# Layer 0 of a graph network: low sums through one bank, node ids in the other, packed count bounds

## The reference

```python
agg = segment_sum(x[src], dst, num_segments=12500)
h = x @ W_self + (agg * inv_deg[:, None]) @ W_neigh + b   # inv_deg = 1 / max(count of dst, 1)
# relu after layers 0 and 1; layer 0 takes layernorm(x)
x = x + h2                                                # the third layer's h
# routed: weights = LN(x) @ wr + br; the upper half of the nodes gets
# (gelu(LN(x) @ w1 + b1) @ w2 + b2) * weight; all rows: processed + LN(x) + x
```

## Time and profile before

| | |
|---|---|
| Median of 3 runs | 6063.86 us |
| The profiled execution | 6064.39 us, of which its span 6062.2 us |
| TensorE matmul, weight loads | 4166.2 us (69%), 2675.0 us (44%) |
| VectorE | 2811.4 us (46%) |
| ScalarE | 1056.5 us (17%) |
| GpSimd | 3912.0 us (65%) |
| Granted TensorE clock, mean | 0.862 |
| One-hots of layers 0 and 2 (L1155) | 3584 operations, 1013.8 us |
| One-hots of layer 1 (L1148) | 408 operations, 282.3 us |
| The chain that ended last | PE 24%, issue 23%, POOL 22%, DMA 9%, VectorE's sequencer 9%, VectorE 9% |

### The profile page before, as it was taken

The page is one execution under the profiler, slowest core; times in us unless marked ns, Lnnn a source line. Parts: engine busy times, 40 slices in busy tenths (PEclk is TensorE's granted clock), DMA queues, the critical chain, the costliest instruction groups (busy, mean ns, idle before and its releaser), DMA issues.

```text
span 6062.2 us, 112776 instructions
## 1 busy us (share of the span) xinstructions
PE 4166.2 (69%) x20492; PEld 2675.0 (44%) x20878; DVE 2811.4 (46%) x8126; ACT 1056.5 (17%) x2551; POOL 3912.0 (65%) x4094
## 2 busy tenths in 40 slices
PE   0444566666666667845778766666569999889992
PEld 0122233333333335523556433333257887667772
DVE  7223455555554445512222333344234445666666
ACT  7000011111111112200000100111012223334440
POOL 0777566665544447667777777776777765777760
PEclk9867788888888889976889988888689999999996
DMA  7555455555544446656777666666567775666655
GB/s 243 156 156 145 125 161 165 166 153 152 149 127 133 135 135 182 177 153 186 230 235 246 205 180 181 185 186 171 158 205 221 232 225 154 175 174 176 170 152 173
DMA packets 565085, 1065.85 MB, mean 176 GB/s; under 512 B 154587, under 2 KB 361983, under 8 KB 558527
## 3 DMA queue, kind: packets, MB, share of 16 engines
q0 software_dynamic: 261376, 803.21, 46.2%
q10 hardware_dynamic: 196564, 228.51, 11.0%
q1 hardware_dynamic: 106987, 32.54, 2.3%
HBM read 928.09 MB, written 135.83 MB: 175 GB/s over the span
## 4 chain that ended last, share of the span: by engine, by line
PE 24%; issue 23%; POOL 22%; DMA 9%; DVEq 9%; DVE 9%; ACT 2%; ACTq 1%; POOLq 0%; SPq 0%
POOL gath L619 22%; DMA gath<-table,idx_ring 7%; PE agg L826 6%; PE y L903 4%; PE hid L893 3%; DVE onehot L1155 3%; PE agg L828 3%; DVEq L1155 2%; DVEq L1214 2%; PE lo L765 2%; PE y L678 1%; DMA idx_ring<-idx_dram 1%; DVEq L1258 1%; PE count_ps L765 1%; ACTq L1502 1%
## 5 line engine op out<-in xcount | busy, mean ns | idle before, releaser
L619 POOL DMA_INDIRECT gath<-table,idx_ring x4084 | 3910.5, 958 | 1986.6 <-issue 1380.9
L826 PE MATMUL agg<-gath,onehot 128*128 x4831 | 1980.4, 439 | 985.0 <-SPq L546 799.6
L1155 DVE TENSOR_SCALAR onehot<-iota_row,window_base,dst_f 128x128 f32 x3584 | 1013.8, 360 | 1276.4 <-PE agg L828 478.3
L826 PEld LDWEIGHTS agg<-gath,onehot 128*128 x5216 | 560.4, 107 | 2122.0 <-issue 1788.3
L828 PE MATMUL agg<-gath,onehot 128*128 x3264 | 969.0, 297 | 184.6 <-SPq L546 139.9
L1148 DVE TENSOR_TENSOR onehot<-count_ps,dst_f 128x512 f32 x408 | 282.3, 692 | 827.7 <-PE agg L828 714.7
L903 PE MATMUL y<-w_sb,hidT 128*128 128x256 f32 x1568 | 368.6, 389 | 26.4 <-ACT hidT L1666 25.8
L828 PE MATMUL hid<-gath,onehot 128*128 x924 | 297.8, 322 | 122.4 <-SPq L546 105.6
L828 PEld LDWEIGHTS agg<-gath,onehot 128*128 x3264 | 338.6, 104 | 83.5
L828 PE MATMUL lo<-gath,onehot 128*128 x1028 | 342.0, 333 | 44.4 <-issue 18.9
L893 PE MATMUL hid<-featT,w_gnn 128*128 128x128 f32 x3136 | 366.9, 275 | 0.0
(11 more groups left out here) (182 smaller groups left out, 3962.1 us busy)
## 6 DMA issues: line engine op xcount, KB each, us to landing
gath<-table,idx_ring POOLq DMA_INDIRECT x4084
dense<-counts_dram ACTq DMA_DIRECT2D x50, 1024.0 KB, 6.4
table<-split ACTq DMA_DIRECT2D x194, 192.0 KB
counts_dram<-dense ACTq DMA_DIRECT2D x16, 1600.0 KB, 9.0
rows_f<-y ACTq DMA_DIRECT2D x194, 128.0 KB
dense<-rows_f ACTq DMA_DIRECT2D x48, 512.0 KB, 9.4
table<-gath ACTq DMA_DIRECT2D x24, 768.0 KB, 3.6
xb<-x ACTq DMA_DIRECT2D x97, 128.0 KB
```

The lines of the kernel that those rows point to most:

```text
L619: g.indirect_dma_start(gath[:, j, 0:PARTS * D], None, table[layer][:, :], bass.IndirectOffsetOnAxis(ap=idx_ring[:, h, i:i + 1], axis=0)).t ...
L826: mm(agg[p][:, 0:2 * D], oh, tile_rows[:, :, 0:2 * D], start=False, **flags)
L1155: last = v.tensor_scalar(onehot[:, bass.ds(pair, GROUP), :][:, j, :], iota_row[:], window_base[:, col(w)], dst_f[:, bass.ds(tiles, GROUP)] ...
```

## The change

Three edits, all in layer 0. (1) Low sums: both parities use one bank `lo0`; ScalarE copies it to `lo_sb[p]` in SBUF at the start of its slot (`lo_copied`); TensorE zeroes the bank for the next window only after that copy, and VectorE's `mean_done` reads the copy. (2) The half of `hid` that comes free takes the node ids, so that layer 0 makes a block's one-hots as layer 1 does. (3) The bounds of two groups are packed into one word (`group_pairs`), and each word's end is kept in a register for the next window, so that a turn of four windows needs 5 loads in place of 16. Beside them TensorE's `layer_product` waits for `self_ready` in place of `lo_ready`.

```diff
+        group_pairs = sb("group_pairs", [1, COUNT_GROUPS // 2 + 1], I32)
+        lo_sb = [sb(f"lo_sb{p}", [P, D + 1]) for p in range(2)]
...
-        agg_lo = [lo0[:], hid[:, 0, :]]
+        agg_lo = lo0[:]
-        window_ids = [count_ps[:, p * P:(p + 1) * P] for p in range(2)]
+        window_ids = [None if bank is None else [bank[:, p * P:(p + 1) * P] for p in range(2)]
+                      for bank in (hid[:, 0, :], count_ps[:], None)]
...
+        def group_bounds(eng):
+            ends = []
+            def end_of(value):
+                return eng.snap(value, min_val=0, max_val=TILES - 1)
+            def both_groups(turn, j):
+                def packed(k):
+                    return eng.value_load(group_pairs[0:1, col(turn * 4 + k)], min_val=0,
+                                          max_val=2 ** (2 * TILE_BITS) - 1)
+                if j == 0:
+                    ends[:] = [end_of(packed(0) >> TILE_BITS)]
+                here = packed(j + 1)
+                first, mid, end = ends[0], end_of(here & (2 ** TILE_BITS - 1)), end_of(here >> TILE_BITS)
+                ends[:] = [end]
+                return (first, mid), (mid, end)
+            return both_groups
...
                 if phase == 1 and (not isinstance(n, int) or n):
-                    pe.wait_ge(lo_ready, n)
+                    pe.wait_ge(self_ready, n)
...
                 if layer == 0:
-                    mm(agg_lo[p][:, 0:1], zeros[:], ones_bf[:, 0:1], start=True, **free)
+                    if not isinstance(n, int) or n:
+                        pe.wait_ge(lo_copied, n)
+                    mm(agg_lo[:, 0:1], zeros[:], ones_bf[:, 0:1], start=True, **free)
...
-                if layer == 1:
-                    v.tensor_scalar(window_ids[p], iota_row[:], window_base[:, col(w)], None,
-                                    ALU.add).then_inc(ids_ready, 1)
-                    dve.wait_ge(ids_ready, w - (DENSE - 1))
+                ids = window_ids[layer] and window_ids[layer][p]
+                if ids is not None:
+                    v.tensor_scalar(ids, iota_row[:], window_base[:, col(w)], None, ALU.add).then_inc(ids_ready, 1)
+                    dve.wait_ge(ids_ready, w + ((NT - DENSE) * layer + 1))
                     dve.sem_inc(dve_turn, 1)
...
-                    if layer == 1:
+                    if ids is not None:
                         v.tensor_tensor(onehot[:, bass.ds(pair, GROUP), :],
-                                        window_ids[p].unsqueeze(1).to_broadcast([P, GROUP, P]),
+                                        ids.unsqueeze(1).to_broadcast([P, GROUP, P]),
...
-                dve.wait_ge(agg_ready, n + 1)
-                v.tensor_scalar(deg[0:r, :], agg_lo[p][0:r, D:D + 1], 1.0, None, ALU.max).then_inc(deg_ready, 1)
+                dve.wait_ge(lo_copied, n + 1)
+                v.tensor_scalar(deg[0:r, :], lo_sb[p][0:r, D:D + 1], 1.0, None, ALU.max).then_inc(deg_ready, 1)
...
+                v.tensor_scalar(group_pairs[0:1, 1:COUNT_GROUPS // 2 + 1], group_tiles[0:1, :, 1], TILE_BITS, None,
+                                ALU.logical_shift_left).then_inc(groups_ready, 1)
+                dve.wait_ge(groups_ready, 9)
+                v.tensor_tensor(group_pairs[0:1, 1:COUNT_GROUPS // 2 + 1], group_pairs[0:1, 1:COUNT_GROUPS // 2 + 1],
+                                group_tiles[0:1, :, 0], ALU.bitwise_or).then_inc(groups_ready, 1)
...
+                    act.wait_ge(agg_ready, n + 1)
+                    if not isinstance(n, int) or n >= 2:
+                        act.wait_ge(mean_ready, n - 1)
+                    a.copy(lo_sb[1 - p][0:r, :], agg_lo[0:r, 0:D + 1]).then_inc(lo_copied, 1)
```

More of the change, by code:

```diff
@@ L87, in gnn_ffn_program @@
     COUNT_LOOPS = [(COUNT_AT, COUNT_END, 4), (COUNT_END, LAST_LOOPED, 2)]
+    TILE_BITS = TILES.bit_length()
     DENSE_LOOPS = [(DENSE_AT, DENSE_LAST, 2), (CLEAN, LAST_LOOPED, 2)]
@@ L301, in gnn_ffn_program @@
         lo_added = sem("lo_added")
+        lo_copied = sem("lo_copied")
         mid_added = sem("mid_added")
@@ L720, in count_ends, with count_group @@
                 nc.tensor.transpose(count_ps[0:1, 0:P], ends_count, ident[:]).then_inc(group_T, 1)
-            def count_group(g):
-                lo, end = pe_groups(g)
+            def count_group(g, bounds):
+                lo, end = bounds
                 (_, mid), _ = sub_spans(pe, lo, end, 2)
@@ L826, in block_products @@
                         mm(agg[p][:, 0:2 * D], oh, tile_rows[:, :, 0:2 * D], start=False, **flags)
-                        low = agg[p][:, 0:D] if layer else agg_lo[p][:, 0:lo_cols]
+                        low = agg[p][:, 0:D] if layer else agg_lo[:, 0:lo_cols]
                         last = mm(low, oh, tile_rows[:, :, 2 * D:2 * D + lo_cols], start=False, **flags)
@@ L847, in _ @@
                                    for blocks in (PAIRS - DENSE, PADDED_BLOCKS)] for layer in range(1, LAYERS)]
-            def pe_groups(g):
-                return [pe.value_load(group_tiles[0:1, col(g + i)], min_val=0, max_val=TILES - 1) for i in range(2)]
+            pe_groups = group_bounds(pe)
             def slot_layer0(w, half, p, part):
@@ L862, in slot_layer0 @@
                 if part and part[0] == 0:
+                    bounds = pe_groups(part[1], part[2])
                     first_half, *counting = [step for j in range(2) for step in
-                                             count_group(part[1] * 8 + (part[2] * 2 + j))]
+                                             count_group(part[1] * 8 + (part[2] * 2 + j), bounds[j])]
                     first_half()
@@ L1178, in mean_done @@
                 mean, inv = feat[p][0:r, :], inv_deg[0:r, col(n)]
-                v.tensor_scalar(mean, agg_lo[p][0:r, 0:D], inv, None, ALU.mult).then_inc(lo_added, 1)
+                v.tensor_scalar(mean, lo_sb[p][0:r, 0:D], inv, None, ALU.mult).then_inc(lo_added, 1)
                 dve.wait_ge(lo_added, n + 1)
@@ L1211, in aggregate_done @@
                                        ).then_inc(feat_ready if layer < 2 else o_ready, 1)
-            def dve_groups(g):
-                return [dve.value_load(group_tiles[0:1, col(g + i)], min_val=0, max_val=TILES - 1) for i in range(2)]
+            dve_groups = group_bounds(dve)
             def split_sources():
@@ L1229, in split_sources @@
                                 ALU.add).then_inc(groups_ready, 1)
-                v.memset(group_tiles[0:1, 0:1], 0).then_inc(groups_ready, 1)
+                v.memset(group_pairs[0:1, 0:1], 0).then_inc(groups_ready, 1)
                 dve.wait_ge(groups_ready, 7)
@@ L1242, in split_sources, with count_onehots @@
                 dve.wait_ge(group_T, 1)
-                v.tensor_copy(group_tiles[0:1, 1:COUNT_GROUPS + 1], count_ps[0:1, 0:COUNT_GROUPS]
+                v.tensor_copy(group_tiles[0:1, :, :].rearrange("p g t -> p (g t)"), count_ps[0:1, 0:COUNT_GROUPS]
                               ).then_inc(groups_ready, 1)
                 dve.wait_ge(groups_ready, 8)
+                v.tensor_scalar(group_pairs[0:1, 1:COUNT_GROUPS // 2 + 1], group_tiles[0:1, :, 1], TILE_BITS, None,
[3 more added lines that the diff above has]
+                                group_tiles[0:1, :, 0], ALU.bitwise_or).then_inc(groups_ready, 1)
+                dve.wait_ge(groups_ready, 10)
                 dve.sem_inc(count_copied, 2)
-            def count_onehots(g):
-                lo, end = dve_groups(g)
+            def count_onehots(g, bounds):
+                lo, end = bounds
                 (_, mid), _ = sub_spans(dve, lo, end, 2)
@@ L1255, in tile_onehots @@
                     slot = dve.snap((t + g) % COUNT_RING)
+                    tile = nc.s_assert_within(
+                        dve.snap(t), 0, TILES - 1,
+                        skip_runtime_bounds_check_because="tiles are counted from the sorted edges, below TILES")
                     dve.wait_ge(count_used, t + 2)
@@ L1280, in slot_layer0 @@
                 if part and part[0] == 0:
+                    bounds = dve_groups(part[1], part[2])
                     first_half, *counting = [step for j in range(2) for step in
-                                             count_onehots(part[1] * 8 + (part[2] * 2 + j))]
+                                             count_onehots(part[1] * 8 + (part[2] * 2 + j), bounds[j])]
                     first_half()
```

6 lines of the change are left out of this document (3 added, 3 removed).

## The result

The changed kernel took 5869.28 us, the median of 4 runs (5863.12 to 5874.99), the kernel before 6061.81 us in 4 runs on the same chip (6059.19 to 6067.04): a ratio of 0.9681, 95% interval 0.9664 to 0.9698, 192 us less. The forecast was 5873.

A forecast was written before the change was run, and what follows sets the result against it. VectorE's stream was taken to bound windows 6 to 69, gathers windows 70 to 97. Savings of 135 (late), 48 (early), 5, 3 and 1 us, less 1 for set-up, sum to 191: 6064.4 - 191 = 5873 us, range 5805 to 5965.

The forecast's parts named there:

- VectorE as the bound of the late stage: Layer 0, windows 22 to 69: VectorE's stream, sequencer included, sets the pace of these 1065 us; TensorE comes next.
- The late stage: Windows 22 to 69 of layer 0: VectorE's stream 149 us shorter (84 + 91 - 26), nine tenths reaching the end, 135 us.
- The blocks: One operation for a block's four one-hots in layer 0: 0.44 us saved per block, bounds 0.30 and 0.72.
- The loads: Packed bounds on VectorE in layer 0: 2.75 fewer register loads a window, 1.9 us saved each, bounds 0.9 and 2.2.
- The early stage: Windows 6 to 21 of layer 0: VectorE's stream 65 us shorter, 62 us of room above the gathers, 48 us taken.
- Setup, the first six windows, the last 28: Set-up costs 1 us; up to window 5, 3 and 5 us saved; windows 70 to 97, bound by gathers, 1 us saved.
- The copy costs nothing: ScalarE's added copy of low sums, about 0.40 us per window, is hidden by TensorE's products; about 1 us a window otherwise.
- The stops stay: The 15 stops of 5.7 to 6.7 us where VectorE's counting loop jumps back remain, the loop fetched anew each turn.
- Had they gone: Rival: VectorE's stops at the counting loop's jumps back go as well, 15 x 5.8 = 87 us more, 5786 us; chance 9 in 100.
- TensorE takes over early: Rival, counting stages: TensorE gives back only half of what VectorE saves, about 95 us, 5969 us; chance 12 in 100.
- One bank slower: Rival: ScalarE copies late, TensorE stands and GpSimd behind it; 3 us exposed per window, 6167 us; chance 3 in 100.
- nothing: Rival: VectorE's savings turn into waits for TensorE at the same places, no measurable change; chance 2 in 100.

The follow-up runs named there:

- f4: VectorE's loops over windows 6 to 69 of layer 0 hold two windows a turn instead of four, on the kernel before: 6016.78 us, ratio 0.9913.
- g1: Changed kernel with VectorE's loops over windows 6 to 69 holding two windows a turn instead of four, quick chip: 5838.75 us, 0.9627 of the kernel before.
- e3_bank: Kernel before with only the one bank for low sums and ScalarE's copy of it, slow chip: 7478.26 us, ratio 0.9992.
- f3b_copy_twice: Changed kernel with ScalarE copying the low sums out of the one bank twice per window of layer 0: 5875.15 us, 0.9689 of the kernel before.
- e4_selfwait: Kernel before with TensorE's layer_product of layer 0 waiting for self_ready in place of lo_ready, slow chip: 7463.02 us, ratio 0.9974.
- f0_after: The changed kernel itself, unedited, on a slow chip: 7280.31 us against 7454.13 for the kernel before, ratio 0.9772.

## Why the prediction was right, step by step

**VectorE as the bound of the late stage: right.** Each part that shortens its stream shortens the stage, the parts add up there (69 + 42 of 118), what the halved loop gives back to VectorE reaches the end whole (f4 and g1), and the edits of TensorE's and ScalarE's handoff alone (e3_bank, f3b_copy_twice) do nothing; e4_selfwait's 19 us are unexplained.

**The late stage, 149 us of VectorE times nine tenths: 150 instead of 135, by two errors of opposite sign.** The blocks were sized too small: in a row they are 0.65 us closer (1.41 to 0.76), not 0.44, near the upper bound of 0.72; that is for blocks in a row, and for one that stands alone the spacing can't be read so. The row of layer 1 that gave 0.99 us for two blocks held 0.30 us of idle time that layer 0 does not have. The loads were as forecast (the gap 3.60 to 1.4 to 2.0). Added up from the view of waits, VectorE's busy time with the idle time that it owes to itself was 543.1 + 423.6 us before and is 471.3 + 300.9: 194 us less, not 149, and more than the 183 us that the prediction named as the best case (its own upper bounds, 192 x 0.72 + 48 x (2.2 - 0.35), add up to 227; 183 is TensorE's room). Beside the earlier trace rows the larger rows of that sum before are

```profile
DVE onehot L1155 <- issue: 110.5, 166, 5.1
DVE split L1121 <- ACT split L1503: 52.9, 48, 3.4
```

Its waits for others went from 80.2 to 126.1 us, 46 more (`rest` for ScalarE, 22.5, is the largest new one). So by this view 150 of 194 us reached the end, 0.77 and not nine tenths, and what was lost went into VectorE's waits for ScalarE (57 us more), not for TensorE, which the prediction had as the next in line. "issue" also holds waits for a semaphore that the sequencer does by itself, so the 194 is good to some tens of us, and the 0.77 rests on this view alone. There is no one share for the stage either: the smaller cuts of f4 and g1, 40 and 37 us by the same sum, came off the end whole. That the forecast of this stage was close is therefore in part luck.

One term put at nothing was small but real: VectorE's read of the low sums from `lo_sb` in SBUF is shorter than the one from the bank, 0.13 us a window where the prediction had 0.1 either way. Before and after:

```profile
L1179 DVE TENSOR_SCALAR feat<-lo,inv_deg x49: 483/484/485, 429.7 to 2562.6; 128x256 f32<-128x256 f32 x49
```

```profile
L1206 DVE TENSOR_SCALAR feat<-lo_sb,inv_deg x98: 348/353/557, 424.6 to 2382.8; 128x256 f32<-128x256 f32 x97, 84x256 f32<-84x256 f32 x1
```


**The early stage, 48: the step that failed, 29.6.** The room over the gathers (62 us) was taken for room that VectorE could use up. VectorE's busy time with the idle time that it owes to itself fell by more than the 65 us forecast, by 86 (280.8 + 166.9 to 240.7 + 120.7), but a third of it reached the end and not three quarters. The view of waits of the changed kernel in 714 to 1175:

```profile
DVE dense L1293 <- PE count_ps L757: 60.5, 32, 6.2
...
PE agg L853 <- SPq L571: 41.8, 15, 7.1
POOL gath L644 <- PE lo L855: 36.1, 21, 7.4
```

and of the kernel before in 723 to 1213:

```profile
POOL gath L619 <- PE lo L828: 44.4, 16, 9.9
...
PE agg L826 <- SPq L546: 22.9, 10, 5.9
...
POOL gath L619 <- PE hid L828: 18.8, 11, 5.0
...
DVE dense L1258 <- PE count_ps L732: 13.8, 12, 2.9
```

VectorE's saving turned into 47 us more of its own wait for TensorE, and TensorE's into 19 us more for the gathers (the wait that SyncE's queue passes on), while GpSimd still waits 36 us for TensorE (63 before): the three hand the wait round before a stage reaches the pace of its gathers. Where the last two of the four stops stand, the chain of waits of the changed kernel runs over the landing of a gather instead:

```profile
1052.07 7.62 DMA gath<-table,idx_ring
1147.88 6.92 DMA gath<-table,idx_ring
```

That the room is not VectorE's to use is shown most plainly by the halved loop: of 14 us less on VectorE 10 reach the end before the change, of 17 after it 4. That two parts which save 30 and 39 us alone save 50 together points the same way, within its noise.

**Setup, the first six windows, the last 28: right** (8.5 for 8; 1 us the other way).

**The copy costs nothing: right**, by e3_bank and f3b_copy_twice. That its cover is TensorE's products and transposes was argued; the runs show only that there is at least 0.27 us of it.

**The stops stay: right**, 15 of 5.6 to 6.7 us for a body of 503 instructions as for one of 631. The Trainium skill (Runtime: NRT & Kernel Launch, Instruction fetch mechanics) gives most engines 512 instructions and says that a taken branch out of the two-page window stalls: the stops agree with the window, and 503 being under 512 was no guard. Had they gone, it would hardly have been 87 us: the 4 of the early stage are worth little after the change. Taking out all 15 by the halved loop, with its costs, gave 50 us before the change and 30 after it.

**The signs.** As forecast: VectorE's busy time (-188 for -180), the one-hots at 0.69, the gap before the first counting one-hot, later stretches unchanged within 4 us, GpSimd's waits for TensorE (-148 for "over 150", just short), TensorE's waits for ScalarE's copy (1.5 us in all). Missed: blocks 0.76 apart, not 1.0; TensorE's waits for VectorE 164 us, not well under 150.

**The rivals.** "TensorE takes over early" is, with the gathers behind it, what happens in the early stage, not in the late one. "One bank slower" and "nothing" fall with e3_bank, f3b_copy_twice and the result.

## What to carry to other kernels

Room over a resource's pace is not room that the bound engine can use: where three engines wait for each other in turn, find the share by a cut of known size, stage by stage, before multiplying. Here the halved loop shows it: all of the cut came off the late stage and, after the change, a quarter off the early one. The size of such a cut is what the engine gets back, not what was taken out: of 65 us of stops it got back 40. Take the spacing of the new operation from a stretch where nothing stands between two of them. A stop at every jump back of a loop is worth one look at the instruction queue: halving the number of windows in VectorE's loop body, with one register load more in four windows, took 30 us off a kernel of 5869.

## What the runs showed of the hardware

**A long loop pays for its jump back, by its length.** On the quick chips VectorE's bodies of four windows (631 and 503 instructions as built) stop 5.6 to 6.7 us at each of 15 jumps; with two windows VectorE is idle at most 0.31 us at any of the 31 jumps, and the instruction queue's packets go from 122 (before) to 30 and from 106 (changed) to 29, of 8 KB each. No loop between these lengths was tried, so where the limit lies is open.

**A register load on VectorE's queue has no fixed price.** It took 0.30 to 0.32 us in most places of the kernel before (median 311 ns of 188 loads), and up to 1.6 us at the start of a loop turn in g1_unroll2 and f4_before_unroll2.

**VectorE reads a 128x256 f32 operand faster from SBUF than from PSUM,** in the one pair that this case has: 353 ns for 484, for the same operation by a per-row scalar.

**The same kernel took 23% longer on three of the four chips, where sequencers were slow.** VectorE's operations and the gathers take what they took (in f0_after the 128x512 one-hots 692 ns for 691 on the mean, a gather 954 ns in both), but many register and branch instructions on the queues take 0.70 us, singly or in runs. TensorE's matmuls are longer there as well: in f0_after it is busy 4570.2 us for 4099.8, at a mean granted clock of 0.799 for 0.865. How the lost time divides between the two, and whether the lower clock follows from the longer idle times, was not tested. For one line, VectorE's loop over blocks, the changed kernel on the first chip and then f0_after (durations min/median/max in ns):

```profile
L1192 DVEq FUSED_REGOPS  x196: 51/52/82, 1192.7 to 2089.4; - x196
```

```profile
L1192 DVEq FUSED_REGOPS  x197: 2/51/728, 1449.3 to 2661.8; - x197
```

The medians are equal; the maximum is not. Over the whole of f0_after's trace 939 register, arithmetic and branch instructions on VectorE's queue and 1407 on TensorE's took over 0.5 us (median 0.70), in the changed kernel's first trace none. What makes them slow is open. The waits in f0_after's late stage show whom it hits:

```profile
POOL gath L644 <- PE lo L855: 507.9, 71, 16.4
...
DVE dense L1293 <- issue: 288.5, 159, 8.9
```

So the same change gave 192 us on one chip and 174 on another (0.9681 and 0.9772), and the shorter loop 30 us and nothing.
